# Causal mask of the row maxima inside VectorE's reduction, and routing weights repeated over partitions by DMA

## The chip, the cores and the metric

One core of a Trainium2 chip runs the whole program in one launch. The metric is the time on the device in microseconds (us), less is better. The kernel before takes 837.76 us as the median of three runs (836.80 to 838.21).

## What is computed

Two sequences of 1024 tokens with 128 features, in float32, go through four residual blocks. Each block is x + f(layernorm(x)):

```python
x = x + attention(layernorm(x), W_qk, W_out)    # 16 heads of 64, keys serve as values, causal
x = x + mixture(layernorm(x), ...)
x = x + state_space(layernorm(x), ...)
x = x + mixture(layernorm(x), ...)              # the same weights
```

The attention: q and k are the two halves of x @ W_qk, scores are q k / 8, entries above the diagonal are replaced by the lowest float, then softmax over keys, and the output is attn @ k. The mixture:

```python
router_logits = sigmoid(x @ gate_w + gate_b)                      # 16 experts
expert_values, expert_indices = top_k(router_logits, k=2)
expert_values = expert_values / sum(expert_values)
all_outputs = (silu(x @ experts_wg) * (x @ experts_wu)) @ experts_wd    # every expert, inner size 64
return x + shared_mlp(x) + sum(expert_values * all_outputs[expert_indices])
```

## The kernel before

Tokens lie transposed (features on partitions) for the matmuls. A float32 operand that needs full precision is kept as a high part and a low part, and a product is three matmuls (high x high, high x low, low x high).

**Attention** (about 23 to 506 us of the span) works on 16 units, one for each pair of heads in each sequence. Two heads share the 128 partitions of an operand, so that most matmuls come in twos (l = 0, 1). For one unit the scores of the next are prepared: `ROUNDS` is an order written out by hand in which TensorE runs score pieces S0 to S8 of the unit and the pieces M0 to M9 of the maxima of the next one, between them the value products (`outputs`, L638). All pieces use three PSUM pairs in turn (`ring_uses`, `pair`, `pair_free`): a piece waits until the piece three uses before it was read, by ScalarE's exponential (L448) if it was an S, by VectorE's reduction (L487) if it was an M. M0 to M9 (`max_scores`, L578) hold approximate scores of 128 queries in rows with up to 512 keys; a fill whose last block of keys is the diagonal one (8 of them, in M0 twice, M1, M2, M5, M8 twice and M9) gets its causal mask by four more bf16 matmuls (L585: mask x identity, added in PSUM). VectorE reduces both heads of a fill in one instruction (L487) into `half_max`, joins the halves (L494) and turns them into rows (L499); a score piece adds the negated row maximum by a matmul (L620) before the exponential. For unit 0 all ten M pieces run ahead of the rounds. `set_up` makes the constants on GpSimd during the first layernorm.

**Mixture** (506 to 649 us and 712 to 833 us). The tokens are in four groups of 512, and each group has nine steps: eight steps of two experts (64 + 64 inner columns fill 128 partitions) and a last one for the shared network. In a step g TensorE projects gate (`g_ps`, L844 to L846) and up (`u_ps`, the same lines), ScalarE takes the silu (L957), GpSimd multiplies by the routing weights (`prod`, L1120), VectorE by the up-projection (`hid`, L1018), and two steps later TensorE projects down into `acc` (L854). The routing weights of a step, one row for each of the two experts, must stand on 64 partitions each: `spread` (L865) does it by one matmul of a selection matrix `f.sel` with `f.wt`, which holds the weights of 16 experts as high part in rows 0 to 15 and low part in rows 32 to 47. It is issued one step ahead into one PSUM bank `wb_ps`, and ScalarE copies it to one of two buffers `wb` (L948).

What prepares the next group (layernorm, routing) and finishes the last one is strewn between the steps by `interleave`, on each engine after the step that `PREPARE` and `FINISH` name, counted from the first step of the group. The routing chain on VectorE is `natural`, `route1` to `route3` (top 2, shares, L1055 to L1076, the last of which makes `w`); then TensorE transposes w (`turn_w`, L938, at -3), ScalarE copies the high part (`w_high`, L992, at -2), and VectorE subtracts for the low part (`w_low`, L1079). For group 0 turn_w stands inside step 0. The SP queue loads weights at the beginning; in the second mixture it stores each finished group of the output, in order. PSUM holds eight banks, of which the mixture uses all.

Of the kernel before, what the change touches and what calls it, by code (L numbers as in the profile page):

```python
# [24 lines left out]
P = 128  # L25
# [213 lines left out]
def attention(nc, k, w_qk, load_x, load_w_out):  # L239
# [3 lines left out]
    with Scope(nc, "at") as s:  # L243
# [16 lines left out]
        eye2, mask2 = s.sb("eye2", [P, 2, P], BF16), s.sb("mask2", [P, 2, P], BF16)  # L260

# [65 lines left out]
        def set_up(pool):  # L327
# [4 lines left out]
            pool.wait_ge(consts, 3)  # L332
# [19 lines left out]
        with nc.Block() as block:  # L352
# [123 lines left out]
            def _(dve):  # L476
# [34 lines left out]
                queries_low(0)  # L511
                for m in range(NMAX):
# [5 lines left out]
                dve.wait_ge(consts, 9)  # L518
# [26 lines left out]
            def _(pe):  # L545
# [23 lines left out]
                def max_scores(unit, m):  # L569
# [5 lines left out]
                    for i, a, b, at in MAX_FILLS[m]:  # L575
                        diag = b == i + 1
                        for l in range(2):
                            last = pe.matmul(out[:, l, at:at + (b - a) * P], qh[u][rows(l), i * P:(i + 1) * P],  # L578
                                             kh[u][rows(l), a * P:b * P], start=True, stop=not diag)
                            if not diag and (i, a, b, at) == MAX_FILLS[m][-1]:  # L580
                                last.then_inc(max_ready, 1)
                        for h in range(2 if diag else 0):
                            o = at + (i - a) * P
                            for l in range(2):
                                last = pe.matmul(out[:, l, o:o + P], eye2[rows(l), h, :], mask2[rows(l), h, :],  # L585
                                                 start=False, stop=h == 1)
                                if h == 1 and (i, a, b, at) == MAX_FILLS[m][-1]:
                                    last.then_inc(max_ready, 1)
# [68 lines left out]
                pe.wait_ge(consts, 9)  # L657
# [35 lines left out]
BUFS = 3  # L693
LAST = STEPS - 1
# [5 lines left out]
               low=-13, logits=-10, sigmoid=-9, natural=-8, route1=-8, route2=-7, route3=-6, turn_w=-3,  # L700
               w_high=-2, w_low=-3)
# [68 lines left out]
def mixture(nc, tag, k, f, source, source_ready=None, load_x=None, weights=None, next_norm=False, store=None, ahead_of=None):  # L770
# [9 lines left out]
    with Scope(nc, tag) as s:  # L780
        g_ps, u_ps, wb_ps, acc, misc = s.ps("g", RING), s.ps("u", RING), s.ps("wb"), s.ps("acc"), s.ps("misc", 2)
# [4 lines left out]
        wb = [s.sb(f"wb_copy{r}", [P, BANK]) for r in range(2)]  # L786
        wb_copied = s.sem("wb_copied")
        g_ready, u_ready, wb_ready = s.sem("g_ready"), s.sem("u_ready"), s.sem("wb_ready")
# [14 lines left out]
        route_step, w_ready, wt_ready, wt_high, wt_low = [  # L803
            s.sem(n) for n in ("route_step", "w_ready", "wt_ready", "wt_high", "wt_low")]
        if weights:
            raw = {n: s.sb(f"raw_{n}", [P, EXPERTS + 2, INTER]) for n in ("wg", "wu")}
            gate_raw = s.sb("gate_raw", [P, EXPERTS])
            sel = s.sb("sel", [P, EXPERTS // 2, P])
            iota_i = s.sb("iota_i", full, I32)
            loaded, split, padded, low_split, iota_made, sel_made, const_done = [  # L810
                s.sem(n) for n in ("loaded", "split", "padded", "low_split", "iota_made", "sel_made", "const_done")]
# [6 lines left out]

        def ahead(g):

            return g < NSTEPS and g % STEPS < LAST

# [14 lines left out]
        with nc.Block() as block:  # L837
            @block.tensor
            def _(pe):
# [19 lines left out]
                def spread(g):  # L859

                    n, st = divmod(g, STEPS)
                    if st == 0:
                        pe.wait_ge(wt_low, n + 1)
                    wait(pe, wb_copied, LAST * n + st)
                    pe.matmul(wb_ps[:, :], f.sel[:, st, :], f.wt[:, cols(n)],  # L865
                              start=True, stop=True).then_inc(wb_ready, 1)

# [726 lines left out]
```

## Time and profile before

| | us |
|---|---|
| median of three runs | 837.76 |
| the profiled execution | 837.44 |
| its span | 835.7 |
| TensorE busy | 767.2 (92%) |
| VectorE busy | 447.3 (54%) |
| ScalarE busy | 422.0 (50%) |
| GpSimd busy | 441.0 (53%) |
| mean granted clock of TensorE | 0.965 of full |

PE is TensorE (matmuls), PEld its weight loads, DVE VectorE, ACT ScalarE, POOL GpSimd, SP the queue that issues DMAs. A row of a timeline gives start, duration, engine, source line, operation, output and inputs with their sizes, how many instructions are merged (x2), and, in brackets, how long the engine was idle before and what released it. Matmuls overlap, so the time between two starts is what one costs. A row of a group gives the same for all instructions of a line, with busy time, mean duration in ns and the idle time ahead of them by releaser. A number with a leading point is in us.

### The profile page before, as it was taken

To read this page: it belongs to the slowest core of one execution; us is meant where nothing else is said; L and a number is where in the kernel's file an instruction comes from. 1 tells how busy PE (TensorE), PEld (TensorE's weight loads), DVE (VectorE), ACT (ScalarE), POOL (GpSimd) and SP (SyncE) were. 2 spreads that over 40 slices of the span, in tenths; PEclk is the share of its full clock that TensorE was granted. 3 is DMA by queue.
4 is the path that set the end of the run, shared out by engine and by line. 5 is a ranking of instruction groups with operands and counts; after the bars stand their busy time and mean duration, and the time that the engine had idled before them with its cause. 6 is when DMAs were issued, how large, how long until landed. Compare 5 with 4: busy or idle time off the path is not lost. (4 is left out here: it accounts for less than half of the span.)

```text
span 835.7 us, 15021 instructions
## 1 busy us (share of the span) xinstructions
PE 767.2 (92%) x6024; PEld 516.6 (62%) x6024; DVE 447.3 (54%) x856; ACT 422.0 (50%) x548; POOL 441.0 (53%) x320
## 2 busy tenths in 40 slices
PE   2699999999999999999999989999998856689998
PEld 2465655656565565656556548877887522667887
DVE  5755565556456555645655502655554775655442
ACT  2355545554554555455555442467555650376542
POOL 3266685666658557656855683143433453143443
PEclk9899999999999999999999999999999885899999
DMA  2000000000000000000000006100000000000000
GB/s 63 7 1 2 8 1 2 7 2 1 9 2 1 8 1 8 1 2 2 1 2 26 2 1 147 23 1 1 1 1 1 2 0 0 1 1 13 15 0 26
DMA packets 18964, 8.15 MB, mean 10 GB/s; under 512 B 7952, under 2 KB 18768, under 8 KB 18896
## 3 DMA queue, kind: packets, MB, share of 16 engines
q1 hardware_dynamic: 18896, 7.20, 3.3%
q8 instruction: 48, 0.79, 0.4%
q14 instruction: 20, 0.16, 0.1%
HBM read 6.15 MB, written 1.05 MB: 9 GB/s over the span
## 5 line engine op out<-in xcount | busy, mean ns | idle before, releaser
L373 POOL TENSOR_TENSOR all_x<-all_x,at_probs 128x1024 f32<-128x1024 f32 (+3 forms) x128 | 220.0, 1718 | 36.8 <-ACT at_probs L448 22.1
L487 DVE TENSOR_REDUCE at_half_max<-at_ring 128x2 f32<-128x1024 f32 (+1 forms) x192 | 177.2, 955 | 115.8 <-PE at_ring L585 101.9
L448 ACT ACTIVATE at_probs<-at_ring 128x1024 f32<-128x1024 f32 x144 | 147.2, 1023 | 123.4 <-PE at_ring L620 122.0
L1120 POOL TENSOR_TENSOR m_prod<-m_gate,m_wb_copy 128x512 f32<-128x512 f32 x64 | 82.0, 1286 | 115.8 <-ACT m_gate L957 113.3
L638 PE MATMUL at_out<-at_probs,at_k_nat 128*64 128x512 f32 (+3 forms) x768 | 140.3, 494 | 1.1 <-DVE a_attn_t L508 0.9
L373 POOL TENSOR_TENSOR all_x<-at_probs 128x768 f32<-128x768 f32 (+1 forms) x32 | 67.0, 2095 | 133.8 <-ACT at_probs L448 133.6
L638 PEld LDWEIGHTS at_out<-at_probs,at_k_nat 128*64 128x64 f32 x768 | 49.2, 136 | 68.2 <-issue 62.9
L1018 DVE TENSOR_TENSOR m_hid<-m_prod,m_u 128x512 f32<-128x512 f32 x64 | 43.9, 687 | 79.1 <-POOL m_prod L1120 69.6
L611 PE MATMUL at_ring<-at_qh,at_kh 64*128 64x512 f32 (+3 forms) x384 | 77.9, 402 | 3.0 <-DVE at_m_rows L499 2.6
L957 ACT ACTIVATE m_gate<-m_g 128x512 f32<-128x512 f32 x72 | 43.1, 599 | 73.6 <-PE m_g L846 73.3
L854 PEld LDWEIGHTS m_acc<-rest_wd,m_hid 128*128 128x128 f32 x576 | 74.7, 191 | 5.9
L620 PE MATMUL at_ring<-at_m_rows,at_ones_r 64*128 64x512 f32 (+3 forms) x384 | 76.1, 391 | 0.0
L854 PE MATMUL m_acc<-rest_wd,m_hid 128*128 128x128 f32 x576 | 75.1, 274 | 0.0
L578 PE MATMUL at_ring<-at_kh,at_qh 64*128 64x512 f32 (+3 forms) x384 | 67.9, 383 | 4.4 <-DVE at_half_max L487 2.8
L615 PE MATMUL at_ring<-at_qh,at_kl 64*128 64x512 f32 (+3 forms) x384 | 67.1, 345 | 0.0
L613 PE MATMUL at_ring<-at_ql,at_kh 64*128 64x512 f32 (+3 forms) x384 | 66.9, 344 | 0.0
L611 PEld LDWEIGHTS at_ring<-at_qh,at_kh 64*128 64x128 f32 x384 | 36.5, 187 | 41.7 <-issue 37.2
L578 PEld LDWEIGHTS at_ring<-at_kh,at_qh 64*128 64x128 f32 x384 | 38.6, 187 | 21.8 <-issue 19.7
L439 ACT ACTIVATE at_inv<-at_misc 128x512 f32<-128x512 f32 x32 | 19.1, 598 | 61.9 <-PE at_misc L651 61.9
L480 DVE TENSOR_TENSOR at_ql<-at_ring,at_qh 128x1024 fp32r<-128x1024 f32 x16 | 19.6, 1225 | 55.1 <-ACT at_qh L424 55.1
L948 ACT ACTIVATE m_wb_copy<-m_wb 128x512 f32<-128x512 f32 x64 | 38.0, 593 | 6.5 <-POOL m_prod L1120 3.4
L615 PEld LDWEIGHTS at_ring<-at_qh,at_kl 64*128 64x128 f32 x384 | 36.4, 186 | 4.2
(202 smaller groups left out, 1355.9 us busy)
## 6 DMA issues: line engine op xcount, KB each, us to landing
all_x<-in_L_attn_a_x SPq DMA_DIRECT2D x8, 256.0 KB, 4.0
at_w_raw<-in_L_attn_a_W_qk SPq DMA_DIRECT2D x8, 128.0 KB, 2.5
out<-all_x SPq DMA_DIRECT2D x4, 256.0 KB, 2.4
a_room<-in_L_attn_a_W_out SPq DMA_DIRECT2D x1, 512.0 KB, 4.5
m_raw_wg<-in_L_ffn_experts_wg SPq DMA_DIRECT2D x1, 512.0 KB, 4.9
m_raw_wu<-in_L_ffn_experts_wu SPq DMA_DIRECT2D x1, 512.0 KB, 4.1
rest_wd<-in_L_ffn_experts_wd SPq DMA_DIRECT2D x1, 512.0 KB, 4.2
rest_w_in<-in_L_attn_b_W_in SPq DMA_DIRECT2D x1, 256.0 KB, 4.2
```

Source lines behind the costliest of these rows:

```text
L373: return pool.tensor_tensor(sums[:, :, a * P:b * P], left, right, ALU.add)
L448: act.activation(probs[:, :, slot * BANK:(slot + 1) * BANK], pair("S", unit, slot)[:, :, :], ACT.Exp, scale=BETA).then_inc(exp_done, 1)
L487: last = dve.reduce_max(half_max[:, :, i, int(a > 0)], pair("M", unit, m)[:, :, at:at + (b - a) * P], AX.X)
L578: last = pe.matmul(out[:, l, at:at + (b - a) * P], qh[u][rows(l), i * P:(i + 1) * P], kh[u][rows(l), a * P:b * P], start=True, stop=not diag)
L611: pe.matmul(to[l], kh[u][rows(l), keys], qh[u][rows(l), q], start=True, stop=False)
L613: pe.matmul(to[l], kh[u][rows(l), keys], ql[u][rows(l), q], start=False, stop=False)
L615: pe.matmul(to[l], kl[u][rows(l), keys], qh[u][rows(l), q], start=False, stop=False)
L620: last = pe.matmul(to[l], ones_r[rows(l), :], m_rows[u][rows(l), q], start=False, stop=True)
L638: last = pe.matmul(out_ps[rows(l), o:o + (b - a) * P], k_nat[g % 3][:, j, rows(l)], probs[:, l, at:at + (b - a) * P], start=(j == 0), stop ...
L854: last = pe.matmul(acc[:, t * P:(t + 1) * P], hid[g % BUFS][:, t * P:(t + 1) * P], f.wd[:, st, :], start=(st == 0 and t == 0), stop=(st == ...
L1018: dve.tensor_tensor(hid[r][:, :], left[:, :], u_ps[g % RING][:, :], ALU.mult).then_inc(hid_ready, 1)
L1120: pool.tensor_tensor(prod[g % BUFS][:, :], gate[g % BUFS][:, :], wb[(LAST * n + st) % 2][:, :], ALU.mult)\
```

## The change

In attention the maxima are no longer masked on TensorE. A new constant `after_query` is zero in 384 columns and holds the causal mask of a diagonal block in the last 128; for a diagonal fill VectorE runs, for each of the two heads, one instruction that adds the mask to the PSUM data in place and takes the row maximum as its accumulator.

In the mixtures the spreading matmul, its PSUM bank, ScalarE's copies, the low part and the selection matrix go. `f.wt` now holds one group's weights in 16 rows of float32. The SP queue stores them to a buffer off chip, waits until they have landed, and loads for each step two rows, each repeated over 64 partitions, into one of four buffers; GpSimd's product waits for the loads. turn_w and w_high move to five steps ahead of the group, from three and two. In the second mixture the output store of a group comes on SP behind the first four steps' loads of the next.

```diff
+            pool.memset(after_query[:, :], 0.0).then_inc(consts, 1)
+            pool.wait_ge(consts, 4)
+            pool.affine_select(out=after_query[:, BANK - P:BANK], in_=after_query[:, BANK - P:BANK], compare_op=ALU.is_ge,
+                               fill=MASKED, base=0, pattern=[[-1, P]], channel_multiplier=1).then_inc(consts, 1)
...
                     for i, a, b, at in MAX_FILLS[m]:
-                        last = dve.reduce_max(half_max[:, :, i, int(a > 0)], pair("M", unit, m)[:, :, at:at + (b - a) * P],
-                                              AX.X)
+                        w, out = (b - a) * P, int(a > 0)
+                        if b <= i:
+                            last = dve.reduce_max(half_max[:, :, i, out], pair("M", unit, m)[:, :, at:at + w], AX.X)
+                            continue
+                        for l in range(2):
+                            sums_ps = pair("M", unit, m)[:, l, at:at + w]
+                            last = dve.tensor_tensor_reduce(
+                                out=sums_ps, in0=sums_ps, in1=after_query[:, BANK - w:BANK],
+                                scale=1.0, scalar=MASKED, op0=ALU.add, op1=ALU.max,
+                                accum_out=half_max[:, l, i, out:out + 1])
                     last.then_inc(max_taken, 1)
...
-                        for h in range(2 if diag else 0):
-                            o = at + (i - a) * P
-                            for l in range(2):
-                                last = pe.matmul(out[:, l, o:o + P], eye2[rows(l), h, :], mask2[rows(l), h, :],
-                                                 start=False, stop=h == 1)
...
-               low=-13, logits=-10, sigmoid=-9, natural=-8, route1=-8, route2=-7, route3=-6, turn_w=-3,
-               w_high=-2, w_low=-3)
+               low=-13, logits=-10, sigmoid=-9, natural=-8, route1=-8, route2=-7, route3=-6, turn_w=-5, w_high=-5)
...
-                    if g > 0 and ahead(g + 1):
-                        spread(g + 1)
...
                         emit("turn_w", 0, "first")
-                        spread(0)
-                        spread(1)
                         emit("logits", 1, "first")
...
-                    if ahead(g + 1):
-                        copy_weights(g + 1)
...
+                        wait(act, wt_stored, 16 * n)
+                        act.activation(f.wt[:, :], misc[1][0:EXPERTS, :], ACT.Copy).then_inc(wt_done, 1)
...
-                        pool.wait_ge(wb_copied, LAST * n + st + 1)
+                        q = LAST * n + st
+                        pool.wait_ge(wb_loaded[q % SPREAD], 32 * (q // SPREAD + 1))
...
+                    def spread(n, st):
+
+                        q = LAST * n + st
+                        wait(sp, weighted, q - SPREAD + 1)
+                        for e in range(2):
+                            sp.dma_start(wb[q % SPREAD][e * INTER:(e + 1) * INTER, :],
+                                         wt_far[n % 2, 2 * st + e, :].partition_broadcast(INTER))\
+                              .then_inc(wb_loaded[q % SPREAD], 16)
...
+                    for n in range(GROUPS + 1):
+                        if n < GROUPS:
+                            sp.wait_ge(wt_done, n + 1)
+                            sp.dma_start(wt_far[n % 2, :, :], f.wt[:, :]).then_inc(wt_stored, 16)
+                            sp.wait_ge(wt_stored, 16 * (n + 1))
+                            for st in range(SPREAD):
+                                spread(n, st)
+                        if n and store is not None:
+                            sp.wait_ge(acc_used, n)
+                            sp.dma_start(grp(store, n - 1), grp(k.x, n - 1)).then_inc(stored, 16)
+                        for st in range(SPREAD, LAST if n < GROUPS else 0):
+                            spread(n, st)
```

## Rows read from the trace of the kernel before

**Rows 1.** The page's busy line; then busy time by window, with granted clock.

```profile
PE 767.2 (92%) x6024; PEld 516.6 (62%) x6024; DVE 447.3 (54%) x856; ACT 422.0 (50%) x548; POOL 441.0 (53%) x320
...
core 0: us, PE busy (x) PEld busy (x) DVE busy (x) ACT busy (x) POOL busy (x), PEclk, DMA share, GB/s
90.00:200.00 110.00, 110.00 (x1026) 65.30 (x1024) 60.25 (x67) 59.26 (x69) 70.18 (x46) 1.00 0.01 4
560.00:600.00 40.00, 38.17 (x228) 31.68 (x228) 21.28 (x65) 26.45 (x40) 15.36 (x12) 1.00 0.00 1
542.80:546.20 3.40, 3.40 (x12) 2.26 (x10) 0.69 (x1) 3.34 (x4) 0.66 (x1) 0.51 0.02 5
```

**Rows 2.** Timeline of TensorE in one attention unit: M1, M3, what follows M9.

```profile
309.04 0.40 PE L578 MATMUL at_ring<-at_kh,at_qh 64*128 64x512 f32 x2
...
309.49 1.08 PE L638 MATMUL at_out<-at_probs,at_k_nat 128*64 128x512 f32 x4
...
312.95 0.73 PE L578 MATMUL at_ring<-at_kh,at_qh 64*128 64x512 f32 x4
313.61 1.94 PE L638 MATMUL at_out<-at_probs,at_k_nat 128*64 128x512 f32 x8
...
323.43 0.42 PE L611 MATMUL at_ring<-at_qh,at_kh 64*128 64x384 f32 x2
```

**Rows 3.** Timeline of ScalarE in the same unit, the exponential of S3.

```profile
311.78 1.02 ACT L448 ACTIVATE at_probs<-at_ring 128x1024 f32<-128x1024 f32 x1 [1.49 <-PE at_ring L620]
```

**Rows 4.** VectorE's groups of instructions by line and form, whole kernel.

```profile
L487 DVE TENSOR_REDUCE at_half_max<-at_ring 128x2 f32<-128x1024 f32 x96 | 114.6, 1222 | 32.0 <-PE at_ring L585 18.1 <-PE at_ring L578 13.9
...
L1063 DVE MATCH_VALUE_LOAD m_at_top<-m_top,m_sc 128x8 f32 x32 | 2.4, 75 | 0.0
...
L1445 DVE SCALAR_TENSOR_TENSOR ss_y<-ss_ps,rest_b_C,ss_state 128x512 f32<-128x512 f32 x2 | 1.5, 752 | 0.1
```

**Rows 5.** Timelines of VectorE (unit 0; the M8 of a later unit) and GpSimd.

```profile
30.30 5.27 DVE L487 TENSOR_REDUCE at_half_max<-at_ring 128x2 f32<-128x768 f32 x6
...
322.16 1.02 DVE L487 TENSOR_REDUCE at_half_max<-at_ring 128x2 f32<-128x256 f32 x2 [0.46 <-PE at_ring L585]
...
16.99 6.24 POOL L96 TENSOR_SCALAR a_attn_t<-all_x,at_moments,at_rstd 128x128 f32<-128x128 f32 x8 [4.57 <-POOLq L137]
```

**Rows 6.** Groups by line: the spreading matmul and its copy.

```profile
L948 ACT ACTIVATE m_wb_copy<-m_wb 128x512 f32<-128x512 f32 x64 | 38.0, 593 | 6.5 <-POOL m_prod L1120 3.4 <-PE m_wb L865 2.9
...
L865 PE MATMUL m_wb<-rest_wt,rest_sel 128*128 128x512 f32 x64 | 27.5, 430 | 10.5 <-ACT m_wb_copy L948 7.1 <-DVE rest_wt L1079 3.1
```

**Rows 7.** Timeline of TensorE in a step of the first mixture.

```profile
559.35 0.39 PE L865 MATMUL m_wb<-rest_wt,rest_sel 128*128 128x512 f32 x1
559.58 0.40 PE L844 MATMUL m_u<-all_xhi,rest_wu_hi 128*128 128x512 f32 x1
```

**Rows 8.** Timelines of GpSimd, ScalarE and TensorE at the first mixture's start.

```profile
542.17 1.28 POOL L1120 TENSOR_TENSOR m_prod<-m_gate,m_wb_copy 128x512 f32<-128x512 f32 x1 [7.96 <-ACT m_gate L957]
...
546.10 0.60 ACT L957 ACTIVATE m_gate<-m_g 128x512 f32<-128x512 f32 x1
...
547.58 0.40 PE L844 MATMUL m_u<-all_xhi,rest_wu_hi 128*128 128x512 f32 x1
```

**Rows 9.** Timelines of VectorE and TensorE around w, second and third group.

```profile
557.14 0.23 DVE L1076 TENSOR_TENSOR m_w<-m_parts 128x64 f32<-128x64 f32 x1
...
555.69 0.60 PE L766 MATMUL m_misc<-all_ident,m_before_xn 128*128 128x128 f32 x4
...
584.50 0.23 DVE L1076 TENSOR_TENSOR m_w<-m_parts 128x64 f32<-128x64 f32 x1
...
581.95 0.60 PE L766 MATMUL m_misc<-all_ident,m_before_xn 128*128 128x128 f32 x4
```

**Rows 10.** DMA issues with time to landing; then two windows of loads, GB/s last.

```profile
out<-all_x SPq DMA_DIRECT2D x4, 256.0 KB, 2.4
...
529.75:531.15 1.40, 1.40 (x15) 1.40 (x14) 1.29 (x14) 0.00 (x0) 0.00 (x0) 1.00 0.19 44
519.15:520.50 1.35, 1.35 (x15) 1.35 (x14) 0.00 (x0) 0.00 (x0) 0.00 (x0) 1.00 1.09 266
```

More of the change, by code:

```diff
@@ L575, in max_scores @@
                     for i, a, b, at in MAX_FILLS[m]:
-                        diag = b == i + 1
                         for l in range(2):
                             last = pe.matmul(out[:, l, at:at + (b - a) * P], qh[u][rows(l), i * P:(i + 1) * P],
-                                             kh[u][rows(l), a * P:b * P], start=True, stop=not diag)
-                            if not diag and (i, a, b, at) == MAX_FILLS[m][-1]:
+                                             kh[u][rows(l), a * P:b * P], start=True, stop=True)
+                            if (i, a, b, at) == MAX_FILLS[m][-1]:
                                 last.then_inc(max_ready, 1)
-                        for h in range(2 if diag else 0):
-                            o = at + (i - a) * P
-                            for l in range(2):
-                                last = pe.matmul(out[:, l, o:o + P], eye2[rows(l), h, :], mask2[rows(l), h, :],
-                                                 start=False, stop=h == 1)
-                                if h == 1 and (i, a, b, at) == MAX_FILLS[m][-1]:
-                                    last.then_inc(max_ready, 1)
                 def turn_max(unit):
@@ L785, in mixture @@
         hid = [s.sb(f"hid{r}", [P, BANK]) for r in range(BUFS)]
-        wb = [s.sb(f"wb_copy{r}", [P, BANK]) for r in range(2)]
-        wb_copied = s.sem("wb_copied")
-        g_ready, u_ready, wb_ready = s.sem("g_ready"), s.sem("u_ready"), s.sem("wb_ready")
+        wb = [s.sb(f"wb{r}", [P, BANK]) for r in range(SPREAD)]
+        wb_loaded = [s.sem(f"wb_loaded{r}") for r in range(SPREAD)]
+        g_ready, u_ready = s.sem("g_ready"), s.sem("u_ready")
         gated, weighted = s.sem("gated"), s.sem("weighted")
@@ L857, in down @@
                     last.then_inc(down_done, 1)
[L859 to L866, printed above, removed]
                 def step(g):
@@ L920, in emit @@
                         pe.wait_ge(before.low, n + 1)
-                        wait(pe, wt_low, n)
+                        wait(pe, wt_done, n)
                         o = misc[1][0:EXPERTS, :]
@@ L1129, in _ @@
                 interleave(("residual",), emit, step)
-            if weights or store is not None:
+            if True:
                 @block.sync
                 def _(sp):
+                    def spread(n, st):
[5 more added lines that the diff above has]
+                              .then_inc(wb_loaded[q % SPREAD], 16)
                     if load_x:
@@ L1148, in _ @@
                         sp.wait_ge(loaded, 16 * 8)
+                    for n in range(GROUPS + 1):
[10 more added lines that the diff above has]
+                            spread(n, st)
                     if store is not None:
-                        for n in range(GROUPS):
-                            sp.wait_ge(acc_used, n + 1)
-                            sp.dma_start(grp(store, n), grp(k.x, n)).then_inc(stored, 16)
                         sp.wait_ge(stored, 16 * GROUPS)
```

64 lines of the change are left out of this document (17 added, 47 removed).

## The prediction

> **What bounds the kernel now.** I read the page's busy shares and the busy time by window first. TensorE is busy 92% of the span; in attention it never stops and runs at full clock, while VectorE and GpSimd are at 55 to 64%. In the mixtures it is busy 95% [rows 1]. So an instruction taken from TensorE is worth its spacing, unless something else ends the wait where it stood. The groups by line and form say who that could be: VectorE's widest 96 reductions were preceded by 32.0 us of waiting, all of it for TensorE, 18.1 for the mask matmuls (L585) [rows 4]. So VectorE follows TensorE today. The timeline then gives spacings, start to start, which are what counts, since one matmul's end overlaps the next one's start. The sum is made against the profiled execution, 837.44 us (span 835.7 and 1.74 around it), 0.3 below the median of 837.76.
>
> **Attention, what goes.** Each of the 16 units drops eight mask groups of four matmuls (L585). A 512-wide fill with its mask takes 309.04 to 309.49, .45 us; without one, two fills take 312.95 to 313.61, .33 each [rows 2]. A mask group costs about .12, eight of them about .95 us a unit. But not all of it comes back. The maxima share three PSUM pairs with the scores, and TensorE waits for a pair. M3 (312.95) starts .15 after the exponential of S3 ends (311.78 + 1.02) [rows 2, 3]; The masks ahead of S3 and S4 (M0's two groups, M1's one) move everything by about .42; the one of M2 only makes the wait for that exponential longer, and M5's, a round on, does the same. Those of M8 and M9 (.23 and .14) count if the pair of M8 is free in time.
>
> **Attention, what comes.** On the eight diagonal fills of a unit VectorE replaces one reduction over both halves by two fused add-and-maximum instructions, each writing an accumulator. No row shows this form. From below: two reductions of half the width. A reduction over 1024 columns takes 1.22 us, and two of 256 together 1.02; a TensorE-bank read with two operands at 512 columns is .75 [rows 4, 5], so a 512-wide fill becomes 2 x .75 less an overlap of .1, plus the read of the accumulator. The nearest row for such a tiny second instruction is the 75 ns load of values [rows 4]. I take about .1 for each, 1.6 at most and 1.3 at least for what is 1.23 now. With widths 128 and 256 (M0, M8) 1.5 where it is 1.02, with 384 (M2, M5) 1.2 where it is .96. Sum: .5 + .5 + .24 x 4 = about 2.0 us a unit, 31 us of VectorE in all, 54% to 57% of the span. From above: if the fused form passes at half speed, a 512-wide fill is 2.6 us and a unit has 7 us more.
>
> Most lies beside other work. M8's reductions start at 322.16 and end at 323.18; the unmasked order would start S8, which needs that pair, at about 323.04 instead of 323.43 [rows 2, 5]. With 1.5 us it can start .15 after 323.45 (first reduction ready .23 earlier), so about 323.6 less the earlier start: S8 gains nothing and loses up to .2. Per unit .42 - .2 = .2 us; 15 units, 3 us. Unit 0 is different: there VectorE goes through all ten fills in one chain and TensorE waits for it. The six instructions from 30.30 take 5.27 without a gap [rows 5]; four fills of that half bring about 1.2 us (.4 to 2.2). The new GpSimd fill and select in the set-up, under 1 us by their neighbours' .3 and .4, end before GpSimd is used again at 16.99 [rows 5]. Attention: -1.8 us, -10 (all masks come back) to +12 (a pair costs 1.9).
>
> **Mixtures, what goes.** 64 spreading matmuls (L865) at a spacing of .23 (559.35 to 559.58) make 14.8 us. TensorE's idle time before them is 10.5 us, 7.1 of it for the one copy bank and 3.1 for the low part of the weights [rows 6, 7]. ScalarE drops 64 copies of .593 us (38 us), VectorE eight subtractions of .68 (L1079), GpSimd, in set-up, the selection tiles, all under other work. Naively: 14.8 + 10.5 = 25.3 us.
>
> **Mixtures, what comes: the start.** Today w is turned, copied high and low, spread and copied again; prod(0) starts at 542.17, and ScalarE's gate(1) at 546.10 behind table loads and a copy [rows 8]. Now the weights are ready at about 539.7, a 32 KB store must land, then two 128 KB loads. A store or load issued by the same queue lands in 2.4 us median (256 KB) [rows 10]. So prod(0) starts at 539.8 + 2.4 + .5 + 2.4 = about 545.1, 2.9 later. Then hid(0) is ready 1.28 + .69 later, at 547.1, and is first waited for by the up-projection of step 2, today at 547.58 [rows 8]: just covered. ScalarE, with two copies less, is earlier with gate(1) and gate(2). Today's pace is lost only if prod(0) starts after about 547.4 (then step 4's up-projection is where it is now). I book the spreads saved there in full. The same cover hides later groups, whose weights are turned five steps ahead (12 us). Two loads and their waits a step on the otherwise empty SP queue, about .5 us issue each, fit in 2.3 us; the output stores of the second mixture now stand behind four loads, and their 2.4 us are hidden save the last, which is where it was.
>
> **Mixtures, what comes: the turn.** This is the new wait. TensorE now stands at turn_w, five steps ahead, until VectorE has w (L1076). In the first mixture's second group w is ready at 557.14 + .23 = 557.37, and TensorE comes to that place at 555.69 today; in its third at 584.73 against 581.95 [rows 9]. Behind turn_w are the next gate projections and so ScalarE, GpSimd and VectorE. What VectorE does before w (hid of three steps, two norms, share 1.25 us, parts) it can begin about 1 us sooner, for two copies of ScalarE gone from its inputs; TensorE comes 2 us sooner. So the wait is about 1.7 for the second group, 2.8 + 1.0 - .2 = 3.6 for the third, 1.6 for the fourth, nearly the same in the second mixture (1.9, 3.0, 1.3, by the same reading of six places in all, of which two are shown). Set against that: a group without routing (the last) gives 8 x .23 + .4 = 2.3. The others give 3.0 to 4.0 (spreads and copy waits) less the wait: 1.6, .3 and 1.8. First mixture 6.0, second 5.1, together 11.1. The clock is a term too: after such an idle stretch the granted clock is .51 of full from 542.80 to 546.20 [rows 1], where eight spacings of .43 for .23 lose about 1.7 us. One such fall more in the kernel, and I book 9.5.
>
> **Loads.** 64 steps x 256 KB = 16.8 MB in all, 256 KB per 2.5 us or 105 GB/s. A row for plain loads gives 266 GB/s in 519.15 to 520.50. But the one load of before that repeats a row over partitions (529.75 to 531.15) moves 44 GB/s [rows 10]. If that is a price per packet (here 512 bytes; 11.7 ns), 2 KB packets go at 175 GB/s, enough; if it is a price per byte of one row, a step's loads take 256 KB / 44 = 6.0 us, too slow. I take the first, since only .19 of the transfer engines' time was used then, which looks like waiting for packets to be made, and keep the second as a rival.
>
> The Trainium skill, "DMA: Bandwidth & Descriptors", section "Latency and other measured facts", has rows at large power-of-two pitches in off-chip memory halve the rate of copies (207 to 103 GB/s), with the cause unverified. Half of 266 is 133 GB/s, 2.0 us a step, which would still fit; a pitch of zero is further along the same line and would speak for the rival. No row here separates them. "VectorE: DVE Perf Modes", section "Two Vector instructions with no wait between them", counts an operation that writes its accumulator as two instructions. No row here shows one. Without it the unit's addition would be 1.2 us less and S8 would start on time, 3 us more gained.
>
> **The sum.** 837.44 - 1.8 - 9.5 = 826.1; I say 826.0.
>
> **Rivals.**
> 1. The turn hardly waits, the clock holds and the masks come back: mixtures give 16 to 19 (25.3 less a start and tail bound by GpSimd's chain), attention 2 to 4: 817 (814 to 820). For it: VectorE is idle 47% of a stretch of the mixture [rows 1], and may run further ahead than I took. Against: w is late today already [rows 9]. Chance .19.
> 2. VectorE's fused form holds the scores. Place: S4 needs M1's pair, at 311.4 in the unmasked order; M1's reductions start at about 309.2, so a 512-wide fill may cost 2.05 us. Up to there it is free, beyond it each unit loses the excess there and again at M4 and S8. At 2.6 us that is .9 at S4, and 1.5 with the later places: 15 x 1.5 + 2 (unit 0) = 24.5, and 837.4 - 9.5 + 24.5 = 852; just past the point, 836. Slower than before from 2.1 us on. For it: no row of this form. Against: a two-operand read of .75. Chance .15.
> 3. Loads of one repeated row go at 44 GB/s. Place: prod waits for wb in each step. 64 x 6.0 = 381 us where the eight groups of nine steps take at least 72 x 2.5 = 180 us: about +180, 1015 us. It decides from 8 x 256 KB in a group of some 25 us, 84 GB/s; at 70 GB/s it is 3.7 us a step, some +30. Chance .18.
> 4. The rest, .48: the forecast, 820 to 833.
>
> The change does what it says in all of these: masks and spreads have rows of their own, and there is no other path for them.
>
> **Range and chances.** 815 to 850 leaves out the third rival (.18) and small ends of the others; the likeliest case's own range is 820 to 833. A measurement of this kernel can tell 0.2%, 1.7 us, from no change. Faster: .48 + .19 = .67. Rival 2 is within 0.2% in .05 and slower in .10; slower in all .28.
>
> **What would show it.** L585 gone, and the two instructions of a 512-wide fill with their read at 1.3 to 1.6 us together; S3 .4 earlier in a unit whose period falls by about .2; M3 still .15 behind ScalarE. Unit 0's second score .5 to 2 us later. prod(0) at about 545 by today's clock; loads landing in 2.2 to 3 us; TensorE idle before L938 (turn_w) for 11 to 14 us in all, in six waits, two of over 3 us, and a granted clock under .9 after one. A mixture step of 2.28 us. A GpSimd wait for a DMA in each step would show rival 3 and VectorE as the releaser of L611 in each unit rival 2. I am wrong in the turn if L938 waits under 5 us.

## The result and the profile after

The changed kernel takes 828.23 us (median of four runs, 827.14 to 829.22); the kernel before took 837.99 beside it. The ratio is 0.9883 (95% interval 0.9868 to 0.9898): 9.8 us or 1.2% faster. The profiled execution took 827.14 us with a span of 825.4, against 837.44 and 835.7. The forecast was 826.0.

So the total is right to 2.2 us, but it is right for partly wrong reasons, as the split shows. I cut both traces at the same places: the last value product, the first matmul of the mixture, its last down-projection, the last matmul of the state space and the last down-projection of all (starts of the matmuls).

| stretch | before, us | after, us | change | predicted |
|---|---|---|---|---|
| up to the last value product of attention (start) | 504.88 | 499.88 | -5.0 | -1.8 |
| first mixture, from its first matmul to its last | 138.85 | 134.77 | -4.1 | -9.5 for both mixtures |
| state space and what lies before it | 62.71 | 62.80 | +.1 | 0 |
| second mixture, from the end of the state space | 124.05 | 122.73 | -1.3 | |

Attention gave nearly three times what I had booked, the mixtures a little over half. This is the page's busy line of the changed kernel, for the first row of [rows 1]:

```profile
PE 740.8 (90%) x5448; PEld 495.9 (60%) x5448; DVE 462.3 (56%) x1232; ACT 390.0 (47%) x483; POOL 439.0 (53%) x316
```

TensorE has 576 matmuls and 26.4 us of busy time less, VectorE 15 us more, ScalarE 32 less. TensorE's share falls from 92% to 90%: it is idle for longer in a shorter span. The list of TensorE's own waits in the mixtures says where (columns: what waited, for what, us in all, times, longest):

```profile
PE m_misc L925 <- DVE m_w L1048: 9.9, 6, 2.5
...
PE m_misc L910 <- DVE all_xlo L756: 4.3, 3, 1.9
...
PE m_u L845 <- DVE m_hid L990: 3.3, 4, 1.6
```

L925 is turn_w, L910 the router's logits, L845 the up-projection (and the gate projection, which waits another 1.8 us in two places). These rows, 19.3 us together, stand in place of the 10.5 us before the spreading matmul in [rows 6] and of 1.0 us for logits and up-projection. The first is the wait that the prediction named.

In a steady attention unit the same three places as in [rows 2] read as follows (timeline of TensorE, the unit that begins at 297.96):

```profile
310.54 0.79 PE L590 MATMUL at_ring<-at_kh,at_qh 64*128 64x512 f32 x4
...
320.44 0.40 PE L590 MATMUL at_ring<-at_kh,at_qh 64*128 64x512 f32 x2
320.99 0.44 PE L616 MATMUL at_ring<-at_qh,at_kh 64*128 64x384 f32 x2 [0.15 <-DVE at_half_max L498]
```

The unit of [rows 2] began at 299.91, by its first transposes (all_ident), so M3 has gone from 13.04 us after its beginning to 12.58, and S8 from 23.52 to 23.03. M3 still starts .14 after ScalarE is through with S3, as in [rows 3]. S8 now waits for VectorE: between M9's matmuls and its own there are .55 us.

The new forms on VectorE, by line and form, whole kernel (where [rows 4] has the one form of before):

```profile
L498 DVE CUSTOM_DVE_ANT_0 at_ring<-at_ring,at_after_query 128x512 f32<-128x512 f32 x64 | 43.2, 718 | 2.9 <-PE at_ring L590 2.9
L498 DVE DVE_READ_ACCUMULATOR2_ANT at_half_max<- 128x1 f32 x256 | 36.4, 142 | 0.0
...
L498 DVE CUSTOM_DVE_ANT_0 at_ring<-at_ring,at_after_query 128x256 f32<-128x256 f32 x64 | 27.1, 466 | 0.0
...
L498 DVE CUSTOM_DVE_ANT_0 at_ring<-at_ring,at_after_query 128x128 f32<-128x128 f32 x64 | 17.5, 316 | 30.2 <-PE at_ring L590 30.2
```

A 512-wide half takes 718 ns, against .75 assumed. The read of the accumulator is a row of its own, 142 ns, but it starts together with the next main instruction: in the timeline the four halves of an M0 and their reads stand between 305.68 and 307.05, 1.37 us, and the two of an M1 between 307.21 and 308.62, 1.41 us. The Trainium skill, "VectorE: DVE Perf Modes", section "Two Vector instructions with no wait between them", counts such an operation as two instructions; the trace agrees, with 256 reads for 256 fused ones. With the attention part alone VectorE is busy for 468.4 us against 447.3 before: the fused forms add 21 us, where the prediction had 31. In the changed kernel the mixtures take 5.4 of this back (the eight subtractions for the low part).

A mixture step is now 2.28 or 2.29 us; where nothing is prepared, in the fourth group, it was 2.50 (620.41 to 622.91 in the trace of before). Gate projection to gate projection, in the timeline of TensorE:

```profile
553.85 0.47 PE L845 MATMUL m_g<-all_xhi,rest_wg_hi 128*128 128x512 f32 x1
...
556.14 0.47 PE L845 MATMUL m_g<-all_xhi,rest_wg_hi 128*128 128x512 f32 x1
```

The beginning of the two mixtures, on GpSimd and on the queue that issues DMAs (timelines, first mixture's product, then second mixture's, then its store and first loads):

```profile
540.48 2.51 POOL L1079 TENSOR_TENSOR m_prod<-m_gate,m_wb 128x512 f32<-128x512 f32 x2 [11.25 <-DMA m_wb<-m_wt_far]
...
728.48 1.26 POOL L1079 TENSOR_TENSOR m_prod<-m_gate,m_wb 128x512 f32<-128x512 f32 x1 [9.18 <-DMA m_wb<-m_wt_far]
...
721.57 0.31 SPq L1119 DMA_DIRECT2D m_wt_far<-rest_wt  x1
725.04 1.08 SPq L1097 DMA_DIRECT2D m_wb<-m_wt_far  x2
```

By the clock of before (this trace runs 5 us ahead here) the first product starts at 545.5; 545.1 was forecast. In the second mixture the store of 32 KB took 3.5 us until the loads could be issued, where the other seven took 1.6.

Last, the loads (page and windows, columns as in [rows 10] and [rows 1]):

```profile
m_wb<-m_wt_far SPq DMA_DIRECT2D x128, 128.0 KB, 2.9
...
537.60:546.40 8.80, 8.11 (x37) 6.17 (x38) 3.17 (x18) 7.41 (x9) 4.32 (x4) 0.82 0.60 180
578.20:582.40 4.20, 4.20 (x18) 3.47 (x19) 1.72 (x6) 2.95 (x4) 0.71 (x1) 0.59 0.04 10
```

While six steps are loaded in a row, 180 GB/s come in. The second window is the stretch behind the longest wait for w: the mean granted clock is .59, since TensorE runs at half clock (1.2 GHz) for most of it.

### The profile page after: what moved, and what is told of

Read it like the earlier page. It is cut to its first block and busy times, and to the rows that moved or that the text cites. A ratio compares the mean times of both kernels' runs of the same rounds, so it can differ in the third digit from the quotient of the medians.

```text
span 825.4 us, 14251 instructions
## 1 busy us (share of the span) xinstructions
PE 740.8 (90%) x5448; PEld 495.9 (60%) x5448; DVE 462.3 (56%) x1232; ACT 390.0 (47%) x483; POOL 439.0 (53%) x316
## 5 line engine op out<-in xcount | busy, mean ns | idle before, releaser
L378 POOL TENSOR_TENSOR all_x<-all_x,at_probs 128x1024 f32<-128x1024 f32 (+3 forms) x128 | 222.9, 1741 | 35.7 <-ACT at_probs L453 21.0
L498 DVE CUSTOM_DVE_ANT_0 at_ring<-at_ring,at_after_query 128x128 f32<-128x128 f32 (+3 forms) x256 | 119.5, 521 | 74.1 <-PE at_ring L590 74.1
L1079 POOL TENSOR_TENSOR m_prod<-m_gate,m_wb 128x512 f32<-128x512 f32 x64 | 81.8, 1283 | 110.6 <-ACT m_gate L936 85.5
L494 DVE TENSOR_REDUCE at_half_max<-at_ring 128x2 f32<-128x1024 f32 x64 | 75.5, 1222 | 12.4 <-PE at_ring L590 12.4
L616 PE MATMUL at_ring<-at_qh,at_kh 64*128 64x512 f32 (+3 forms) x384 | 73.4, 379 | 6.1 <-DVE at_m_rows L512 2.6
L590 PE MATMUL at_ring<-at_kh,at_qh 64*128 64x512 f32 (+3 forms) x384 | 65.3, 389 | 8.7 <-ACT at_probs L453 2.7
L590 PEld LDWEIGHTS at_ring<-at_kh,at_qh 64*128 64x128 f32 x384 | 36.3, 190 | 29.5 <-issue 26.2
```

The costliest lines, as they stand in the source:

```text
L378: return pool.tensor_tensor(sums[:, :, a * P:b * P], left, right, ALU.add)
L494: last = dve.reduce_max(half_max[:, :, i, out], pair("M", unit, m)[:, :, at:at + w], AX.X)
L498: last = dve.tensor_tensor_reduce(out=sums_ps, in0=sums_ps, in1=after_query[:, BANK - w:BANK], scale=1.0, scalar=MASKED, op0=ALU.add, op1= ...
L616: pe.matmul(to[l], kh[u][rows(l), keys], qh[u][rows(l), q], start=True, stop=False)
L1079: pool.tensor_tensor(prod[g % BUFS][:, :], gate[g % BUFS][:, :], wb[q % SPREAD][:, :], ALU.mult)\
```

## The experiments

**Each part alone.** The edits are the parts of the diff before and after the line `RING = 2`.

> The attention part of the change alone (fused masked maxima on VectorE, no mask matmuls for them); the mixtures are those of before. Theory A (as the trace of the changed kernel is read now): attention ends 5.0 us earlier than before (14 steady units of 28.76 instead of 29.23 us, less 1.5 us in unit 0), and that gain does not depend on the mixtures: 833.0 us (832 to 834). Theory B (the prediction's own split): attention gives 1.8 us, the rest seen in the trace belongs to that one execution: 836. Theory C (the two parts share the clock's budget, so that a denser attention costs clock later): 835 to 837 with a lower granted clock in the mixtures.

> The mixture part alone (weights stored off chip and repeated by DMA, turned five steps ahead); the attention is that of before, mask matmuls included. Theory A: 837.8 - 5.3 = 832.5 us, with the same waits for w ahead of the transposes (11 us in six) and two falls of the clock. Theory B (the prediction's split): 828.3. Theory C: the parts are not additive, and this one and the other alone together give 2 us more or less than the 9.8 of both.

Measured: attention alone 832.3 us (ratio .9934, .9917 to .9950), mixtures alone 833.8 (.9947, .9930 to .9963), against 837.8. These are 5.5 and 3.9 us; both together are 9.4, and the changed kernel has 9.8. The parts add up, theory A for both (the mixtures 1.3 us short of it, and with three more falls of the clock than before where it had two), and the prediction's split of 1.8 and 9.5 falls in both places. It is not one execution's chance: the steady unit is 28.76 us in this trace too.

**Where w is transposed.**

```diff
-               low=-13, logits=-10, sigmoid=-9, natural=-8, route1=-8, route2=-7, route3=-6, turn_w=-5, w_high=-5)
+               low=-13, logits=-10, sigmoid=-9, natural=-8, route1=-8, route2=-7, route3=-6, turn_w=-4, w_high=-4)
```

This is turn_m4; turn_m3 has -3 and turn_m6 has -6 in both places.

> The changed kernel with the transposes of w and the copy four steps ahead of the group instead of five; nothing else. Theory A (TensorE waits at the transposes since VectorE's w comes late; one step of 2.28 us later it is there): the waits of 2.1, 2.7, 1.1, 2.0, 2.5 and about 1 us go; of them 1.1 stays in the third group of each mixture and .4 in the second, as a wait of the up-projection for hid, since VectorE itself is behind; without the stalls the clock does not fall in the third group (1.6 us each). 827.9 - 8.5 - 2 = about 817.5 us. Theory B (VectorE's chain is the bound around the preparation, whatever stands where): the stall only moves to the up-projection: 825 to 828. Theory C (the clock falls anyway): 819 to 821.

> The changed kernel with the transposes of w and the copy three steps ahead (the place that the transposes had before); nothing else. Store and loads take about 1.2 + 1.6 + 3.6 us from the transposes, and the product of step 0 would start 6.0 us after them: theory A says some .7 us late, hidden since hid(0) is first needed by the up-projection of step 2: as four steps ahead within 1 us, 817 to 819. Theory B: store and loads need the five steps; with three the product waits for them in each group and drags VectorE along: 822 to 828. Theory C: VectorE's chain is the bound in any case: 825 to 828.

> The changed kernel with the transposes of w six steps ahead instead of five; nothing else. Theory A (w comes when VectorE is through, and TensorE waits from the place of the transposes until then): each of the six waits grows by a step, 2.28 us, 13.7 in all, and the clock falls after most of them, 1.6 us each time: 828.2 + 13.7 + 3 to 6 = 845 to 848, slower than the kernel before. Theory B (the place of the transposes has no weight of its own, VectorE's chain is the bound): 828 to 831.

Measured: 820.46 us at four steps (ratio .9787, .9771 to .9804), 818.70 at three (.9767, .9749 to .9784), 828.23 at five and 846.88 at six (1.0103, 1.0086 to 1.0120). The wait of TensorE for w at six steps (list of waits; the row for five, 9.9 us, stands above), then what is left at four and at three, where that row is gone and the wait for hid, 3.3 us at five, has grown:

```profile
PE m_misc L925 <- DVE m_w L1048: 22.6, 6, 6.5
```

```profile
PE m_u L845 <- DVE m_hid L990: 13.0, 6, 5.3
```

```profile
PE m_u L845 <- DVE m_hid L990: 9.6, 6, 3.5
```

From five to six the time grows by 18.6 us, of which the rows of waits show 22.6 - 9.9 = 12.7, against 13.7 expected; the clock explains most of the rest: 39 gate and up projections at six steps and 16 at five are followed by the next matmul after some .43 us instead of .23, and 23 x .20 makes 4.6 us. Behind the longest wait (6.48 us, before 582.78) the granted clock is .50 of full:

```profile
582.80:586.50 3.70, 3.70 (x12) 2.90 (x13) 0.00 (x0) 1.95 (x3) 0.70 (x1) 0.50 0.04 9
```

So the place has a weight of its own, as theory A has it, and the place of two small pieces of work decides the sign of the whole change: at six steps ahead it is a loss of 1%. From six to five 18.6 us, from five to four 7.8, from four to three 1.8; the last is hardly beyond the scatter, since the four times of each overlap (818.75 to 821.04 and 816.81 to 819.68). The gain from five to four stays 3 us under what theory A expected (817.5), and the 820.46 lies in the range of theory C (819 to 821), but not for its reason: in the third group the clock does not fall any more (1.00 in 578.00 to 582.20 of turn_m4). In the third group of each mixture the stall does move in part, as expected: in turn_m3 the up-projections at 578.1 and 759.3 start 1.35 and 1.09 us after the matmul before them, where .23 is the spacing. No half-clock spacings stand behind these. What both expectations had left out is the start. In turn_m4 the up-projection of step 2 starts 5.2 and 5.7 us after the matmul before it in the two mixtures; in turn_m3 3.9 and 3.7, in the changed kernel .95 and 1.98. There TensorE arrives sooner, and the chain from w through store, loads and product to hid is no shorter. The row of turn_m3 and then the stretch around the same wait in turn_m4, with a granted clock of .50 where the changed kernel has .96 over the same stretch:

```profile
542.57 0.79 PE L845 MATMUL m_u<-all_xhi,rest_wu_hi 128*128 128x512 f32 x1 [3.51 <-DVE m_hid L990]
```

```profile
540.30:547.10 6.80, 4.04 (x14) 3.56 (x15) 4.09 (x21) 1.98 (x3) 3.73 (x3) 0.50 0.52 176
```

That turn_m4 waits longer here than turn_m3 comes mostly from transfers, not from the place: in turn_m4 one of the first two loads landed after 4.3 us (3.0 in turn_m3), and in the second mixture the store after 3.2 (1.6).

Why it arrives sooner is an order on ScalarE's queue. The copy of w at five steps ahead is sorted before the copy of the second group's tokens (four steps ahead), at four and three behind it. In the changed kernel ScalarE stands idle for 11.14 us until TensorE has transposed w, and the tokens' copy, which the logits need, comes behind:

```profile
534.12 0.59 ACT L965 ACTIVATE rest_wt<-m_misc 16x512 f32<-16x512 f32 x1 [11.14 <-PE m_misc L925]
534.62 0.57 ACT L765 ACTIVATE all_xhi<-m_misc 128x512 fp32r<-128x512 f32 x1
```

```profile
535.96 0.41 PE L910 MATMUL m_misc<-all_xhi,rest_gate_hi 128*16 128x512 f32 x1 [1.88 <-DVE all_xlo L756]
```

That row, its like at 722.80 (1.88) and .9 each ahead of the next gate projection are 5.6 us that the prediction did not have. They are not lost in full, since the chain to hid would hold TensorE a little later in any case.

**What the fused form costs.** Expected and edit:

> The changed kernel in which VectorE takes the maxima of the diagonal fills as before, one reduction over both heads, with no mask at all: the causal mask is left out of the maxima (it stays in the scores, so a row's shift is only larger). It measures what the fused form itself costs. Theory A (in a steady unit only the score piece S8 waits for VectorE, by .24 us for M8's pair; unit 0 is VectorE's own chain, 1.2 us longer by the fused form): the unit falls from 28.76 to about 28.5 us and the whole by 14 x .24 + 1.2 = 4.6, from 828 to 823.5. Theory B (S8 is held by ScalarE or by the order, the fused form is free in steady units): 827. Theory C (VectorE's 15 us more are paid in full): 813.

```diff
-                        if b <= i:
+                        if True:
                             last = dve.reduce_max(half_max[:, :, i, out], pair("M", unit, m)[:, :, at:at + w], AX.X)
                             continue
```

Measured: 821.39 us (.9808, .9792 to .9825), 6.8 us less than the changed kernel. The steady unit is 28.36 us, .40 less and not .24. At the same place as above:

```profile
316.11 0.39 PE L590 MATMUL at_ring<-at_kh,at_qh 64*128 64x512 f32 x2
316.33 0.42 PE L616 MATMUL at_ring<-at_qh,at_kh 64*128 64x384 f32 x2
```

S8 follows M9 by .22 instead of .55: .33 us of the .40 is the wait for the pair of M8. Unit 0's first score starts at 41.48, against 42.50 in the changed kernel and 40.98 before. Of that 1.0 us the fused form has .76: from the first matmul of M0 to the first score there are 17.97 us here and before, 18.73 in the changed kernel and with the attention part alone. 14 x .40 + 1.0 is 6.6 of the 6.8. Theory A has the places right and the size of the first too small (.24 for .33, besides .07 elsewhere in the unit). Theory C (VectorE's added time paid in full) falls: VectorE is busy for 20.8 us less here than in the changed kernel (441.5 against 462.3; the 15 us of the expectation were net of what the mixtures save), and TensorE gains 6.8.

It also shows what all eight mask groups were worth: 29.23 - 28.36 = .87 us a unit, near the .95 by spacing. The groups that I had counted make .42 + .23 + .14 = .79, so that .08 is left for those of M2 and M5, which I had booked at nothing.

**One row again and again, or different rows.**

```diff
-                                         wt_far[n % 2, 2 * st + e, :].partition_broadcast(INTER))\
+                                         f.w_in_far[e * INTER:(e + 1) * INTER, :])\
...
+    f.w_in_far = ins["attn_b_W_in"]
```

> The changed kernel in which each of the 128 loads reads 64 different rows of 2 KB (the input matrix of the state space) instead of one row 64 times; the routing weights in the product are thus left out, the bytes, packets, waits and issues are the same. Theory A (price per packet or of the queue, not of the row): packets again every 11.6 ns when four steps are loaded in a row, 2.9 us to landing, and the time within 1 us of the changed kernel's 828. Theory B (reading one row again and again is slower): packets every 7.7 ns as in the plain load of before (266 GB/s), landing .3 to .5 us sooner, some 1 us less in all. Theory C (banks off chip): different rows are slower, over 3.2 us to landing.

Measured: 827.97 us (.9887, .9868 to .9905), the changed kernel's time. Page and window of the same stretch of loads:

```profile
m_wb<-in_L_attn_b_W_in SPq DMA_DIRECT2D x128, 128.0 KB, 2.7
```

```profile
537.80:546.10 8.30, 8.12 (x39) 6.53 (x40) 2.80 (x17) 7.36 (x9) 3.82 (x4) 0.80 0.65 190
```

190 GB/s with different rows and 180 with one repeated row; .2 us in landing. Theory B holds for .2 us of landing and for nothing in the time. So the rival of one slow row is dead for the 2 KB rows of this kernel.

That the price is one for each packet is shown only in part. One repeated row costs 11.4 ns a packet at 2 KB (2048 bytes at 180 GB/s) and 11.7 at 512 bytes (44 GB/s in [rows 10]), so that the prediction's choice gave the right rate. But in the trace of before different rows of 512 bytes came at 222 GB/s, 2.3 ns each, just ahead of that repeated one (window of before):

```profile
529.10:529.60 0.50, 0.50 (x6) 0.47 (x6) 0.44 (x1) 0.00 (x0) 0.00 (x0) 1.00 0.76 222
```

At 512 bytes the repeated row was the slower one by five times, and at 2 KB the two are alike. No run here repeats a short row with nothing else changed, so what the repetition itself costs there is open. The queue is a bound close by, too: where it does not wait it issues a load of 128 KB every .64 us here, which allows 205 GB/s at most (timeline of the changed kernel, 16 loads with a few waits between them):

```profile
536.38 11.89 SPq L1097 DMA_DIRECT2D m_wb<-m_wt_far  x16
```

**The row straight from SBUF.** Besides the lines shown the edit sets turn_w and w_high to -3 and gives `f.wt` a second buffer.

```diff
-                            sp.dma_start(wt_far[n % 2, :, :], f.wt[:, :]).then_inc(wt_stored, 16)
-                            sp.wait_ge(wt_stored, 16 * (n + 1))
...
-                                         wt_far[n % 2, 2 * st + e, :].partition_broadcast(INTER))\
+                                         f.wt[2 * st + e:2 * st + e + 1, n % 2, :].unsqueeze(1).to_broadcast([1, INTER, BANK]))\
```

> Turned three steps ahead, as in turn_m3, and the loads take their row straight from the weights in SBUF (two buffers for alternate groups): no store off chip, no wait for its landing. Theory A (at the start of each mixture the store's round trip of 1.6 to 3.5 us stands in the chain from w to the product of step 0, and TensorE waits 3.9 and 3.7 us for hid(0)): these waits fall to 2.2 and about 1, and 818.7 becomes 814.5 (813.5 to 816). Theory B (a row in SBUF lies in one partition, and reading it 64 times is slower than from off chip): landing over 4 us, the gain goes, 818 to 822, and if it cannot keep up with a step, 830 and more.

> As sbuf_m3, and in the first mixture w of the first group is transposed before step 0's gate and up projections instead of after them (w is ready at 530.0, the transposes stood at 533.5). Theory A: the chain to the product of step 0 starts 1.5 us sooner, TensorE's wait for hid(0) in the first mixture falls by as much: 1 to 1.5 us less than sbuf_m3, about 813. Theory B: that start is by now bound by ScalarE's five table loads of 1.28 us and its gates: no change against sbuf_m3.

Measured: 1171.04 us (ratio 1.398) and 1168.90 (1.396). Theory B, and far beyond its numbers (the earlier transposes in the second of the two are worth 2.1 us there):

```profile
m_wb<-rest_wt SPq DMA_DIRECT2D x128, 128.0 KB, 15.3
```

```profile
560.00:600.00 40.00, 19.25 (x74) 15.31 (x73) 6.00 (x17) 4.06 (x7) 7.54 (x6) 0.71 0.87 32
```

A load lands after 15.3 us, the transfer engines are busy for .87 of the time and move 32 GB/s, and TensorE is busy less than half. This is the prediction's third rival, a transfer that can't keep up with a step, alive in another memory: a step's 256 KB take 8 us instead of 2.3, an estimate of 365 us more in 64 steps, and 352 over turn_m3 were measured. The round trip off chip is not a detour in this kernel but what makes the repetition cheap. The Trainium skill, "DMA: Bandwidth & Descriptors", section "Where 436 GB/s comes from", speaks of sixteen ports into SBUF that make 435 GB/s together; an estimate from that for a row which lies behind one port is 27 GB/s. The run shows 32 with one partition as the source, somewhat more than one port would give by that estimate. That the port is the cause was argued, not tried; nor was a repeated source that is spread over several partitions. Reading SBUF as such is not slow: the output stores, 256 KB from 128 partitions, land in 2.4 us in the kernel before [rows 10].

**Two versions put together.** turn_m3, and in the first mixture w of the first group transposed ahead of step 0's projections; then the same with unmasked maxima.

```diff
+                    if g == 0 and weights:
+                        emit("turn_w", 0, "first")
                     wait(pe, gated, g - RING + 1)
                     up(g_ps[r], f.wg_hi, f.wg_lo, st, n).then_inc(g_ready, 1)
...
-                        emit("turn_w", 0, "first")
+                        if not weights:
+                            emit("turn_w", 0, "first")
                         emit("logits", 1, "first")
```

> turn_m3 (three steps ahead, off-chip store and loads), and in the first mixture w of the first group is transposed before step 0's projections. Theory A (the chain w, copy, store, loads, product, hid sets TensorE's wait of 3.9 us in step 2): 1.5 us less than turn_m3's 818.7: 817.2, where the store lands in 1.6 us in both. Theory B (table loads of ScalarE are the bound of the start): 818.7.

> As m3_early, and the causal mask is left out of the maxima (one reduction over both heads, as in plain_max; the scores are masked as before). If the parts add up: m3_early less the 6.8 us that plain_max gained: 810.4 (809.5 to 811.5). If a denser attention costs clock in the mixtures: 812 to 814.

Measured: 818.21 us (.9768, .9751 to .9785), the same as turn_m3 within what four runs can tell, and 810.71 (.9668, .9652 to .9684). In the first mixture the up-projection of step 2 starts 1.36 us earlier than in turn_m3:

```profile
541.21 0.50 PE L845 MATMUL m_u<-all_xhi,rest_wu_hi 128*128 128x512 f32 x1 [3.33 <-DVE m_hid L993]
```

and that mixture is 2.3 us shorter (129.6 against 131.9, with three half-clock spacings fewer), while the second one, whose program is the same, is 1.7 us longer (118.2 against 116.5), with five more of them near 728 than in turn_m3's trace. That the clock took it back there is what the rows suggest; a single trace of each can't settle it, and the times do not decide between the two theories (817.2 and 818.7). The last version adds up: 818.2 less 7.5, where 6.8 was expected, within the range of 809.5 to 811.5. It is 3.3% under the kernel before, the fastest here.

## Why the prediction was right, step by step

**Attention, what goes** was sized right where it was booked: S3 is .46 earlier (.42 said), M3 stays behind ScalarE. **What comes** was mis-sized upward. A 512-wide fill costs 1.41 us (1.3 to 1.6 said), M0 and M8 1.37 where I took 1.5, and VectorE's addition is 21 us and not 31. The term that failed is the one after it: "so S8 gains nothing and loses up to .2". S8 gains .49 us against its unit's beginning: .38 that M8 has gained before it, and .11 from M8 to S8, where the prediction took .17 of loss and rounded it to .2. M8's fused instructions start .27 sooner after their matmuls than before (.23 said), they take .13 less than said, and TensorE starts .06 after VectorE's last read, not .15. So S8 does wait for VectorE, but a unit's period falls by .47 and not by .2. 14 units of it less 1.5 us at the start make the 5.0. The 1.5 only looks like the 1.2 that was booked: the chain of unit 0, from M0's first matmul to the first score, is .76 longer (17.97 to 18.73), and the other .76 lie ahead of M0, at 23.77 against 23.01. They are not shown to be the change's: in the traces of the other kernels M0 starts anywhere between 22.3 and 23.9.

**Mixtures, what goes**: the spacing of the spread, .22 a step in the fourth group, and the waits for copies are gone as said. But the rows of waits above put 19.3 us where 11.5 stood. The 14.8 us of spreads less these 7.8 are 7.0, against the 5.4 of the table; the clock is in the difference.

**The turn** is right in kind and place: six waits, of 9.9 us in all where 13.1 had been worked out, the longest 2.5 instead of 3.6, since TensorE too arrives later than I took. The signs that were named, 11 to 14 us in all and two waits of over 3, are missed. The place was confirmed in both directions, by turn_m6 and turn_m3. The **clock** term was booked once at 1.6 us; spacings of .43 stand behind the longest wait in both mixtures (five at 579.7, three at 766.6), so that the two mixtures have two more falls and not one. The number of falls differs between executions: the trace of `distinct`, whose program has the same order, has four more than the kernel before. Over the second group's nine steps (first gate projection to first gate projection), in which the third group's w is awaited, the two mixtures are .93 and 1.18 us slower than before, where .3 faster had been said for the first, and one fall for both.

**The start** is where the mixtures' term failed. The store and the loads are as said in the first mixture (.4 late). Two things were not: the copy of w stands ahead of the tokens' copy on ScalarE, which made TensorE wait for its logits, and in the second mixture the store took 3.5 us. "I book the spreads saved there in full" was wrong: over the first group's nine steps the first mixture gained .62 us, where 1.6 was in the sum, and the second lost .17. The third and fourth groups of the first mixture gained 2.35 and 2.04, near the 1.8 and 2.3 of the sum. I had asked what is queued behind TensorE's wait, and not what is queued behind ScalarE's copy that was moved three steps.

**Loads**: the rate that was taken, 175 GB/s, was right, with 11.4 ns a packet against 11.7. The reason is weaker than the number: different rows of 512 bytes in the same trace cost 2.3 ns each, and different rows of 2 KB are as slow as the repeated one, so the 44 GB/s were not those of packets in general.

The errors were 3.2 us too little in attention and 4.1 too much in the mixtures (5.4 by this trace), and so the total came out within 1%: the closeness of 826.0 is luck, and the split is where the reasoning can be judged. The likeliest case's own range, 820 to 833, held the time; the rival in which the fused form holds the scores has its mechanism (S8 waits .33 a unit) but not its sign.

## What to carry to other kernels

A preparatory step that is moved ahead to cover a transfer is also a wait moved ahead: look up when its input is ready, and what stands behind it on each queue that it passes, the copying engine's too. Here five steps ahead gained 1.2%, three gained 2.3% and six lost 1%, with the same work removed. If a matmul only repeats a 2 KB row over partitions, a DMA from off chip can do it for about 11.5 ns a packet; from one partition of SBUF it took five times as long. A softmax's shift need not be the masked maximum: moving the mask gained 5.5 us, and leaving it out there 6.8 more (valid as long as a masked score does not exceed a row's true maximum by so much that its exponentials vanish).

## What the runs showed of the hardware

- Repeated reads of one 2 KB row off chip run at 180 GB/s, of different rows at 190, of one row of one SBUF partition at 32. One repeated row of 512 bytes off chip came at 44 GB/s, different rows of 512 bytes at 222.
- An instruction on VectorE that adds, takes the maximum and accumulates costs 718 ns for 512 columns with one operand in PSUM, and its accumulator's read 142 ns, which lies beside the next one's start.
- The store of 32 KB off chip was over after 1.6 us in seven of eight cases and after 3.5 us in one, the first of the second mixture. At that place it took 3.2 to 3.6 us in six of the nine traces that have this store, and 1.6 in turn_m3, m3_early and `distinct`; at other places five traces have one store each of 1.8 to 3.2. What sets it is open.
